# Routing the first six tiles of a Mixture of Experts in two groups in place of one, with the stores of rows among the last masks

## The reference, cut to what matters

```python
x = x + tanh(g_xattn[0]) * L0_xattn(layernorm(x), ctx_512, ...)   # 16 heads of 8, causal self attention + cross attention
x = x + tanh(g_ffn[0])   * L0_ffn(layernorm(x), ...)

# L0_ffn: 8 experts, the best 2 of each token, capacity 160 rows for each of the two choices
router_probs = softmax(x_flat @ gate_w.T)
top_k_probs, top_k_idx = top_k(router_probs, 2)
for k in range(2):
    onehot  = (top_k_idx[:, k, None] == experts)
    pos     = (cumsum(onehot, axis=0) - 1)[token, its expert]     # a token's place: counts all tokens before it
    valid   = pos < capacity
    disp    = zeros(E, capacity, D).at[eid, pos].add(x_flat)
    out    += weight * expert(disp)[eid, pos]
```

## Time and profile before

| | us |
|---|---|
| three timed runs | 332.91, 335.91, 335.41 |
| their median | 335.41 |
| the profiled execution, first to last instruction (span) | 337.6 |
| TensorE busy | 312.9 (93%) |
| VectorE, ScalarE, GpSimd busy | 220.8, 194.1, 115.7 |

### The profile page before, as it was taken

One profiled execution on the slowest core, in us unless ns is written; L12 is line 12 of the kernel. 1 busy time (PEld: TensorE's weight loads), 2 busy tenths in 40 slices (PEclk: granted clock), 3 DMA queues, 4 the chain that ended last, 5 costly groups with the idle time before them and its releaser, 6 DMA issues.

```text
span 337.6 us, 7474 instructions
## 1 busy us (share of the span) xinstructions
PE 312.9 (93%) x2891; PEld 189.6 (56%) x2891; DVE 220.8 (65%) x532; ACT 194.1 (57%) x410; POOL 115.7 (34%) x200
## 2 busy tenths in 40 slices
PE   8998969989999999899977999999996899999995
PEld 3545733334443434344666677777794357776665
DVE  4998798888989889676242052333321956779665
ACT  3468588978888889787266733323336265512221
POOL 6476732327334333231775003444442211110000
PEclk9999999999999999999997999999999999999999
DMA  7855995940437006240441580000002200000101
GB/s 174 199 110 160 175 213 132 209 90 10 153 110 209 5 5 188 70 124 2 109 157 35 133 212 10 21 18 19 22 12 70 71 0 2 1 2 0 31 3 31
DMA packets 35827, 27.83 MB, mean 82 GB/s; under 512 B 5627, under 2 KB 33070, under 8 KB 35792
## 3 DMA queue, kind: packets, MB, share of 16 engines
q1 hardware_dynamic: 33965, 25.04, 29.7%
q0 software_dynamic: 1280, 1.88, 1.7%
q10 hardware_dynamic: 547, 0.44, 0.5%
HBM read 11.89 MB, written 5.26 MB: 51 GB/s over the span
## 4 chain that ended last, share of the span: by engine, by line
PE 73%; ACT 7%; DVE 6%; issue 5%; POOL 5%; DMA 2%; SPq 0%; DVEq 0%; POOLq 0%; ACTq 0%
PE psum L1682 11%; PE psum L1876 11%; PE psum L1957 8%; PE psum L1624 5%; PE psum L1648 5%; PE psum L1945 4%; PE psum L1864 4%; ACT qk_r L948 3%; PE psum L1814 2%; POOL rows_in L797 2%; PE psum L1651 2%; PE psum L2060 2%; PE psum L2052 1%; PE psum L1575 1%; PE psum L1869 1%
## 5 line engine op out<-in xcount | busy, mean ns | idle before, releaser
L1213 DVE TENSOR_REDUCE nmax<-psum 128x2 f32<-128x1024 f32 (+2 forms) x88 | 102.0, 1216 | 11.6 <-PE psum L1624 10.3
L948 ACT ACTIVATE parts<-psum 128x512 f32<-128x512 f32 (+1 forms) x88 | 45.2, 566 | 8.6 <-PE psum L1648 7.7
L1876 PE MATMUL psum<-p_more,kcat 128*128 128x320 f32 (+2 forms) x160 | 40.2, 396 | 0.9 <-DVE p_more L1346 0.7
L819 POOL DMA_INDIRECT rows_back<-qcat,back_at x24 | 22.9, 952 | 50.3 <-ACT qcat L981 43.1
L1876 PEld LDWEIGHTS psum<-p_more,kcat 128*128 128x128 f32 x160 | 26.1, 190 | 9.1 <-issue 0.9
L1350 DVE TENSOR_TENSOR qcat<-psum,qk_r 128x320 f32<-128x320 f32 (+2 forms) x40 | 16.6, 422 | 22.1 <-ACT qk_r L989 13.5
L989 ACT ACTIVATE qk_r<-psum 128x320 f32<-128x320 f32 (+2 forms) x40 | 15.2, 384 | 24.5 <-PE psum L1876 21.5
L1682 PE MATMUL psum<-parts,v_aug 128*18 128x256 f32 (+1 forms) x352 | 28.5, 369 | 0.0
L1957 PE MATMUL psum<-h_t,kcat 128*128 128x512 f32 x60 | 28.1, 594 | 0.0
L1682 PE MATMUL psum<-qk_r,v_aug 128*18 128x256 f32 (+1 forms) x160 | 27.4, 373 | 0.0
L1648 PE MATMUL psum<-qcat,kcat 64*128 64x256 bf16 x256 | 24.7, 271 | 1.9 <-ACT p_more L948 0.8
(11 more groups left out here) (249 smaller groups left out, 630.4 us busy)
## 6 DMA issues: line engine op xcount, KB each, us to landing
kcat<-parts SPq DMA_DIRECT2D x18, 192.0 KB, 3.8
qcat<-parts SPq DMA_DIRECT2D x21, 128.0 KB, 3.6
kcat<-ones_b SPq DMA_DIRECT2D x8, 192.0 KB, 4.6
kcat<-in_L_ffn_wi_gate_dram SPq DMA_DIRECT2D x6, 256.0 KB, 4.5
kcat<-in_L_ffn_wi_up_dram SPq DMA_DIRECT2D x6, 256.0 KB, 4.8
kcat<-in_L_ffn_wo_dram SPq DMA_DIRECT2D x6, 256.0 KB, 5.0
parts<-in_L_ffn_w_dram SPq DMA_DIRECT2D x3, 512.0 KB, 5.6
rows_in<-zeros SPq DMA_DIRECT2D x1, 1290.0 KB, 5.7
```

The source lines that it names most:

```text
L819: pool.indirect_dma_start(out=rows_back[:, :], out_offset=bass.IndirectOffsetOnAxis(ap=back_at[0:m, e, t:t + 1], axis=0), in_=eo[0:m, e % ...
L948: act.activation(p_slots[u % NPT][:, 0:w], s2_bank(s2_place[u])[:, 0:w], ACT.Exp, scale=SCALE).then_inc(p_in, 1)
L1213: dve.tensor_reduce(dst[:, :, n * g:n * (g + 1)], src.rearrange("p (r q k) -> p r q k", r=PAR, q=n), AX.X, ALU.max, negate=True).then_inc( ...
L1876: ins = pe.matmul(gate_up_bank(i, m)[:, 0:end - first], w_t[e][:, m, f * P:(f + 1) * P], xs_t[:, e % 2, first:end], start=True, stop=True)
```

## The change

Tiles 0 to 5 become two groups. Tiles 0 to 3 (batches 0 and 1), whose attention is long done, are turned from bank 1 right in step 79, and their pieces follow in steps 81, 84, 86 and 88. Tiles 4 and 5 (batch 2) follow from bank 0 in steps 82, 84, 89, 91 and 94. The three small transposes of the router's weights and a bias move to step 82. GpSimd does the first root behind the mask of head 54, the second behind that of head 57, and puts one store behind each of the masks of heads 60 to 63; eight more stores and only then the root of tiles 6 and 7 follow, and their four stores.

```diff
-        EARLY = 3 * QT
-        EARLY_AT = dict(rows=81, project=83, turn=89, router=91, count=94)
+        TILES0 = ((0, 2 * QT), (2 * QT, 3 * QT), (3 * QT, NT))
+        ROUTE_AT = (dict(rows=79, project=81, turn=84, router=86, count=88),
+                    dict(rows=82, project=84, turn=89, router=91, count=94))
+        ROUTE_BANK = (1, 0)
+        EARLY = TILES0[-1][0]
...
-        LG_BANK = [(1, 3), (0,)]
+        LG_BANK = [(1, 1, 3), (0,)]
...
-        COUNT_BANK = [0, 7]
+        COUNT_BANK = [1, 0, 7]
         GW_AT = 2 * P
-        RSTD_AFTER, RSTD_PUT = 3 * H + 2 * QUAD - 1, 7
+        RSTD_AFTER = (54, 57)
+        PUT_AFTER = 60
...
-                if head == RSTD_AFTER:
-                    rstd_group(1, *groups_of(1)[0])
...
+                if head in RSTD_AFTER:
+                    rstd_group(1, *TILES0[RSTD_AFTER.index(head)])
+                if head == PUT_AFTER:
+                    pool.wait_ge(zeroed, 16 * N_ZERO)
+                    pool.wait_ge(put_in, 1)
+                if head >= PUT_AFTER:
+                    put(head - PUT_AFTER)
+
+            for n, (first, end) in enumerate(TILES0):
+                pool.wait_ge(put_in, n + 1)
+                for i in range(2 * first if n else NHEAD - PUT_AFTER, 2 * end):
+                    put(i)
+                if n == 1:
+                    rstd_group(1, *TILES0[2])
...
             take_turned(NPART - 1, bank(0))
+            take_rows_turned(y_t, yt_full, yt_in, ((1, 1, 0, 0, 4),))
             divide_last(TAIL)
...
+            add_projected(1, 1, 0, 0, 4)
+            dve.wait_ge(x1_in, 1)
+            statistics(1, 0, x1_sb)
+            take_rows_turned(y_t, yt_full, yt_in, ((2, 0, 0, 4, EARLY),))
...
+            normalise(1, 0, x1_sb)
             take_values(TAIL + 1)
+            add_projected(2, 0, 0, 4, EARLY)
             dve.wait_ge(x1_in, 2)
+            statistics(1, 1, x1_sb)
+            take_rows_turned(h_t, ht_full[1], ht_dve[1], ((1, 1, 0, 0, 4),))
             divide_last(TAIL + 1)
+            choose(0, 0, *TILES0[0])
+            normalise(1, 1, x1_sb)
+            route(0, *TILES0[0])
             take_values(TAIL + 2)
```

More of the change, by code:

```diff
@@ L415, in groups_of @@
         def groups_of(i):
-            return {0: ((0, 2), (2, 4), (4, 8)), 1: ((0, EARLY), (EARLY, 8)), 2: BACK}.get(i, ((0, 4), (4, 8)))
+            return {0: ((0, 2), (2, 4), (4, 8)), 1: TILES0, 2: BACK}.get(i, ((0, 4), (4, 8)))
         def expert_weights(e):
@@ L774, in add_bias, with put @@
                                    ALU.add).then_inc(xb_in, 1)
+            def put(i):
+                t, k = i // 2, i % 2
+                pool.indirect_dma_start(out=rows_in[0:E * SLOTS, :],
+                                        out_offset=bass.IndirectOffsetOnAxis(ap=put_at[:, k, t:t + 1], axis=0),
+                                        in_=h_rows[:, t, :], in_offset=None, bounds_check=last_slot,
+                                        oob_is_err=False).then_inc(put_out, 16)
             split_before = {}
@@ L1454, in _ @@
             dve.wait_ge(x1_in, 3)
-            statistics(1, 1, x1_sb)
-            normalise(1, 1, x1_sb)
+            statistics(1, 2, x1_sb)
+            normalise(1, 2, x1_sb)
             take_rows_turned(h_t, ht_full[1], ht_dve[1], ((3, 0, 0, EARLY, NT),))
-            choose(0, 1, EARLY, NT)
-            route(1, EARLY, NT)
+            choose(0, 2, *TILES0[2])
+            route(2, *TILES0[2])
             weigh_routed()
@@ new lines, in route_early @@
+                for i, at in enumerate(ROUTE_AT):
+                    first, end = TILES0[i]
+                    place = ROUTE_BANK[i]
+                    if step == at["rows"]:
+                        pe.wait_ge(s1_free, len(pass1) + i)
+                        if i == 1:
+                            pe.wait_ge(in_late, 16 * N_IN_LATE)
+                            for layer in range(2):
+                                pe.transpose(bank(0)[:, GW_AT + layer * E:GW_AT + (layer + 1) * E], gw_rows[:, layer, :],
+                                             ident[0:E, 0:E])
+                            pe.transpose(bank(0)[:, GW_AT + 2 * E:GW_AT + 2 * E + 1], b1_row[:, :],
+                                         ident[0:1, 0:1])
+                        turn_rows(y_sb, y_ready, yt_full, place, first, end)
+                    elif step == at["project"]:
+                        if i == 1:
+                            pe.wait_ge(gw_in, 1)
+                        project_rows(i + 1, place, 0, first, end)
+                    elif step == at["turn"]:
+                        turn_rows(h_sb, h_ready, ht_full[1], place, first, end)
+                    elif step == at["router"]:
+                        route_rows(i + 1, LG_BANK[0][i], first, end)
+                    elif step == at["count"]:
+                        count_rows(i, first, end)
@@ L1988, in _ @@
             turn_weights(1)
-            route_rows(3, LG_BANK[0][1], EARLY, NT)
+            route_rows(3, LG_BANK[0][2], EARLY, NT)
             turn_weights(3)
-            count_rows(1, EARLY, NT)
+            count_rows(2, EARLY, NT)
             turn_weights(3 * E - turned[0])
```

50 lines of the change are left out of this document (5 added, 45 removed).

## The result

The change makes the kernel slower. The changed kernel took 340.45 us (median of 4 runs, 339.49 to 341.18), the kernel before 334.16 (4 runs, 332.88 to 335.91); the ratio is 1.0195, with a 95% interval from 1.0148 to 1.0242. Forecast were 337.1 us and a difference of 1.7; it is 6.3. A second set of runs gave 340.51 against 333.63, ratio 1.0182 (1.0147 to 1.0216). In three runs further down (two of before_six, one of later_still) the clock was low for so much longer that medians and ratios leave them out.

A forecast was written before the change was run, and what follows sets the result against it. Stores delay nothing; the chain runs through the root and normalising of tiles 6 and 7, then TensorE, which also paces the attention pass's end. 1.65 plus 0.1, rounded to 1.7, on 335.4 gives 337.1 us; range 333.4 to 339.6.

The forecast's parts named there:

- Step 84: TensorE's value products wait 1.55 us for GpSimd's mask of head 55; TensorE is 2.05 behind at step 85.
- Steps 85 to 95: Steps 85 to 90 add 0.5 us, steps 91 and 94 give back 0.9; step 95 starts 1.65 later.
- VectorE's added work: VectorE gains 18 rows of about 0.2 us, some 3.5 us in all, most of it in its waits.
- The clock: Rival: the hole in step 84 lowers TensorE's clock, 1.9 us, 339.6 in all; chance 0.18 together with the root held.
- The root of tiles 6 and 7: Stores ahead of it on GpSimd, ending at 172.9, hold this root by about 0.4 or nothing; taken as 0.1 us.
- The sum: 1.65 us at step 95 plus 0.1 for the held root, rounded to 1.7 us slower.
- The median: The 1.7 us difference was put on the median of three timed runs, 335.4, giving 337.1; the profiled execution spanned 337.6.
- The rival with the stall: TensorE's idle 1.97 us at 178.08 and slow weight turns go away with the stores: 333.2 us; chance 0.14.
- Stores beside VectorE's work: GpSimd's stores now run beside VectorE's routing and don't slow it: charged nothing, against some 3 us by the skill's rule.
- the room of 3.5 us: Between the first expert's rows landing at about 187.9 and TensorE turning them at 191.39, some 3.5 us are spare.

The follow-up runs named there:

- before_six: Kernel before with six stores ahead of the root of tiles 6 and 7 in place of seven: 335.65 us, ratio 1.0057.
- later_still: Kernel later with the first group's count one step later again (90) and VectorE's taking of values ahead of the slot numbers: 336.43 us, ratio 1.0055.
- hole_five: Changed kernel with five unread matmuls in TensorE's wait for the mask of head 55 in step 84: 337.45 us, ratio 1.0101.
- both_filled: Kernel both with three unread matmuls in each of TensorE's two gaps of step 84: 336.40 us, ratio 1.0061.
- groups_only: Kernel both with all sixteen stores behind the last mask, none among the masks: 337.18 us, ratio 1.0073.
- later: Kernel both with the first group's turn, router and count one step later each (85, 87, 89): 335.48 us, ratio 1.0038.
- both: Changed kernel with head 55's mask ahead of the first group's root, and tiles 6 and 7's root ahead of the ninth store: 336.26 us, ratio 1.0084.
- before_again: Kernel before, unaltered, profiled a second time: one run of 333.1 us with a span of 331.4.
- after_again: Changed kernel, unaltered, run and profiled again: 340.51 us against 333.63, ratio 1.0182.
- before_root_late: Kernel before with twelve stores ahead of the root of tiles 6 and 7 in place of seven: 342.15 us, ratio 1.0231.
- root_early: Changed kernel with the root of tiles 6 and 7 ahead of the ninth store, not behind the twelfth: 337.45 us, ratio 1.0098.
- mask_first: Changed kernel with the mask of head 55 ahead of the first group's root: 337.92 us, ratio 1.0118.
- before_mask: Kernel before with the root of its six tiles ahead of the mask of head 55: 340.60 us, ratio 1.0194.

## Why the prediction was wrong

The direction was right, and so was the wait in step 84. What failed are two steps of the sum, the clock, put at nothing, and the root of tiles 6 and 7, put at 0.1, and the profile that both were read from; the steps behind 84 were also sized too small.

**Step 84** (forecast 1.55 of waiting, 2.05 behind at step 85). The wait was 1.28, and with the clock up hole_five is at 11.97 - 9.61 = 2.36. This step held in size. Two parts of it didn't. TensorE should have come 0.5 sooner, but step 84 starts where it did (8.66 against 8.69), since its scores wait 0.69 for ScalarE. And the mask, which the forecast made the cause, isn't what sets the 2.36: with it out of the way step 85 starts 0.1 sooner (11.86 in both_filled, 11.85 in groups_only). Turning h in this step sets most of it: in later, one step later, step 85 starts at 10.13, and the pass ends at 29.69 in place of 30.27.

**Steps 85 to 95** (forecast 1.65 at the end). With the clock up it is 30.38 - 27.97 = 2.41, so 0.76 short (3.83 in the profiled execution, with the fall). Of the 0.76, 0.31 was there at step 85. Up to step 90 came 1.02 (18.86 - 15.48 = 3.38) where 0.5 was forecast, with a wait of 0.42 for the choice in place of 0.2 and one of 0.32 for ScalarE that wasn't forecast; the steps behind gave back 0.97, forecast 0.9. VectorE's added work was smaller than charged: 13 rows and 2.7 us by the page of the profile, not 18 and 3.5.

**The clock** was the rival with 0.18 and a price of 1.9; it decided from a gap of 1.97, mine was 0.4 short. This step failed. The fall came in step 84 in both profiles of the changed kernel and cost 1.35 (31.73 - 30.38) to 1.48 (both against groups_only). The length was read from one stall in one trace; the runs have falls behind 0.72 and 1.28, and none behind 0.98 (before_again) or 1.79 (hole_five). In the forecast's own trace TensorE also idles 2.04 from 169.57, longer than the 1.97, and the clock is 1.00 over 171.6 to 180 behind it. The Trainium skill, page "TensorE: Matmul & The Clock Gate", section "What's actually happening", has it that activity lifts a default throttle. The unread matmuls of hole_five agree with that, with 1.00 over 144.8 to 151.6 in place of 0.75 in after_again; the pair both and groups_only shows that the gap in sight isn't all there is to it.

**The root of tiles 6 and 7** (forecast 0.1). This step failed, too: the wait cost 16.12 - 15.42 = 0.70 and the fall behind it 1.11 (2.68 in the second profile). Two errors met. The statistics were placed by a stall of the first profile, 1.7 us too late, which made seven stores look harmless and twelve nearly so; and the end of the stores, 172.9, followed from a first store at 155.7. It came at 160.27. Of these 4.6 us 2.15 are the shift of this execution, 1.3 the slot numbers (ready at 159.18), which are late as TensorE is, and 1.1 the mask of head 60, which stands ahead of it on GpSimd and itself waits for ScalarE until 159.46. before_root_late shows how steep this term is.

**The sum** for the profiled execution, beside the second profile of the kernel before: the spans differ by 339.4 - 331.4 = 8.0. Between step 78 and the contexts lie 2.41 + 1.42 + 0.70 + 1.11 = 5.6 (1.42 is 31.80 - 30.38, from its own rows), in place of the 1.75 forecast; 2.5 of it are falls, charged at nothing. Another 2.6 are there before step 78 (138.25 against 135.68), where nothing was altered and two falls lie, and 0.2 come back behind. Of the 6.3 between the medians, the 5.6 is what the traces tie to the change; the rest stays open.

**The median.** The forecast put a difference on 335.4, a median of three runs; more runs gave medians of 333.6 to 334.6. And it said that the profiled execution was 2.2 over the median, without asking what in the trace made it so. A device time is 1.7 to 1.8 more than its span in every run here, so that execution was at 339.4, 6 over the 333.3 of runs near full clock.

**The rival with the stall** had its cause wrong: the idle 1.97 at 178.08 isn't in the second profile of the same kernel, so there was nothing for the change to remove. In the changed kernel's trace the turns of weights run through from 182.84 on; the forecast had set that down as a sign about the stores, and it isn't one. **Stores beside VectorE's work**, charged at nothing: in root_early the normalising of two tiles takes 0.67 with a store from 173.81 beside it, in both_filled 0.60, also with a store from 173.81, and in mask_first 0.61 with GpSimd idle. That is 0.07 at most, far from what the Trainium skill's page "Advanced Engine Details and Errata", section "Mode Summary", would have made it.

## What to carry to other kernels

Compare the profiled execution with the fastest timed run before reading slack off it: a stall without a named cause moves every later event, and the room of 3.5 us seen here was some 0.15, and where several transfers must land, read the last of them. On an in-order queue that feeds two paths (masks and roots, roots and stores), ask for each item what is queued behind it and in what order the data arrive; one item in the wrong place cost 7 us and more twice here (before_mask, before_root_late), and one in the right place moved the wait to the next path (before_six). Before you blame the item that is waited for last, ask what would be waited for next: taking the mask away bought 0.1 of its 1.28. Where a dense engine gets a gap, price the gap and the fall of the clock behind it as two terms, and try a few unread matmuls that fit into the gap (five won time here, twelve didn't).

## What the hardware showed

Identical programs differ by falls of the granted clock. The one in step 84 is 3.4 us at 1.2 GHz, 0.005 of the mean (in both from about 147.3 to 150.7); behind the wait for tiles 6 and 7 the clock was low for about 6.9 us in after_again and about 10 in before_root_late. In the kernel before the runs at 0.999 to 1.0 took 333.0 to 333.9 with one exception of 335.2 (median 333.3), those at 0.993 to 0.995 took 333.5 to 336.8 (334.9), those at 0.988 to 0.99 335.5 to 336.6. By the traces one fall cost 1.35 to 1.48 in the attention pass and 1.11 among the turns of weights. One indirect store of 128 rows holds GpSimd for 0.97 us and 0.30 pass before the next, so sixteen take 20.4; this pace, not their data, ends them in the kernel before. What made TensorE idle at 169.57 and 178.08 in the first profile stays open. For the first of these stalls the profile does name a releaser, ScalarE's copies (L971): ScalarE starts the copy that ends the wait at 170.96, 1.4 after TensorE's last turn, and VectorE's start at 169.55 is late as well. Both stalls are in one profile of the kernel before and not in the other.
